# Expert weights in six places instead of four, one set of statistics for Mamba's two norms, tanh in place of sigmoid, in an eight-layer network on one core

## What is computed

```python
def _layernorm(x, axis=-1, eps=1e-05):
    m = jnp.mean(x, axis=axis, keepdims=True)
    v = jnp.var(x, axis=axis, keepdims=True)
    return (x - m) / jnp.sqrt(v + eps)
...
# layer 1
r = jax.nn.sigmoid(jnp.einsum('btc,dc->btd', xr, W_r))
...
# layer 2, whose input x is the layernorm above
h = (x - mu) * lax.rsqrt(var + LN_EPS) * ln_g + ln_b
...
return x + out
...
# layer 6
x_in = jax.nn.silu(xz[..., :D]) * jax.nn.sigmoid(xz[..., D:])
...
out = out * jax.lax.rsqrt(jnp.mean(out * out, axis=-1, keepdims=True) + eps) * norm_w
...
# layer 7, for the two best of eight experts of each token
g = jnp.einsum('nd,edf->enf', xt, w_gate) + b_gate[:, None, :]
u = jnp.einsum('nd,edf->enf', xt, w_up) + b_up[:, None, :]
h = jax.nn.silu(g) * u
y = jnp.einsum('enf,efd->end', h, w_down) + b_down[:, None, :]
```

## Time and profile before

| | us |
|---|---|
| median of 3 runs | 1400.7 |
| lowest and highest run | 1398.04 and 1400.92 |
| span of the profiled execution | 1400.6 |
| PE busy in it | 1104.8 (79%) |
| DVE, ACT, POOL busy | 890.9, 630.4, 281.7 |

### The profile page before, as it was taken

How to read it: one execution, slowest core, us unless ns; L and a number is a source line. 1 busy time by engine, 2 the same in 40 slices (tenths; PEclk the granted TensorE clock), 3 DMA queues, 4 the chain that set the end, 5 groups by cost and what they waited for, 6 DMA issues and landing times.

```text
span 1400.6 us, 15057 instructions
## 1 busy us (share of the span) xinstructions
PE 1104.8 (79%) x4959; PEld 698.7 (50%) x4959; DVE 890.9 (64%) x1919; ACT 630.4 (45%) x1194; POOL 281.7 (20%) x258
## 2 busy tenths in 40 slices
PE   4978657767977979686768676799999899897791
PEld 2536312334743634353457442574555556787781
DVE  6787879987558767767635789723735652363432
ACT  3433385424552348634237972273252434542330
POOL 3000113324120002130230244202000032014404
PEclk9999877777989999878889897999999999899996
DMA  8100000003520000000125420370000014468782
GB/s 322 47 0 1 0 0 0 0 1 118 163 61 1 0 0 1 0 0 0 45 92 177 131 74 21 96 224 21 1 1 0 1 63 132 157 214 283 260 277 69
DMA packets 49411, 107.02 MB, mean 76 GB/s; under 512 B 4840, under 2 KB 32368, under 8 KB 48688
## 3 DMA queue, kind: packets, MB, share of 16 engines
q1 hardware_dynamic: 44656, 92.74, 20.7%
q0 software_dynamic: 4096, 8.40, 2.0%
q10 hardware_dynamic: 576, 4.87, 0.8%
HBM read 91.24 MB, written 14.75 MB: 76 GB/s over the span
## 4 chain that ended last, share of the span: by engine, by line
PE 41%; DVE 22%; ACT 13%; issue 9%; POOL 7%; DMA 6%; SPq 1%; DVEq 0%; POOLq 0%; ACTq 0%
PE ps L1920 6%; PE ps L1638 5%; DMA expert_ring<-in_e_dram 4%; PE ps L1586 4%; PE ps L1752 4%; DVE up L1341 3%; PE ps L1858 3%; POOL slots_dram L717 3%; ACT big L957 2%; PE ps L1692 2%; PE ps L1829 2%; PE ps L1958 2%; DVE big L1348 2%; POOL up L727 2%; PE ps L1909 1%
## 5 line engine op out<-in xcount | busy, mean ns | idle before, releaser
L1858 PE MATMUL ps<-big,expert_ring 128*128 128x128 f32 x1160 | 158.0, 286 | 33.6 <-DMA expert_ring<-in_e_dram 20.4
L1858 PEld LDWEIGHTS ps<-big,expert_ring 128*128 128x128 f32 x1160 | 145.2, 199 | 48.0 <-DMA expert_ring<-in_e_dram 26.9
L1341 DVE TENSOR_TENSOR_SCAN up<-cv,big 128x512 f32<-128x512 f32 x128 | 152.5, 1230 | 21.5 <-ACT cv L908 17.4
L660 POOL TENSOR_TENSOR rstd<-ve,nhalf 128x4 f32<-128x4 f32 (+1 forms) x41 | 47.2, 1153 | 577.2 <-DVE ve L1119 470.6
L1752 PE MATMUL ps<-big,consts 128*128 128x512 f32 x256 | 154.3, 735 | 2.4 <-DVE big L1348 2.4
L697 POOL TENSOR_TENSOR big<-big,mt 128x512 f32<-128x512 f32 x64 | 85.8, 1344 | 279.1 <-ACT mt L901 152.6
L1920 PE MATMUL ps<-big,weights 128*128 128x512 f32 x256 | 115.4, 597 | 0.0
L1769 PE MATMUL ps<-q,row_pick 96*128 96x512 bf16 x128 | 54.5, 448 | 76.6 <-DVE big L1348 61.4
L1829 PE MATMUL ps<-expert_ring,big 128*128 128x128 f32 x792 | 107.6, 280 | 5.9 <-ACT big L957 3.6
L1829 PEld LDWEIGHTS ps<-expert_ring,big 128*128 128x128 f32 x792 | 98.9, 195 | 15.3 <-ACT big L957 9.8
L1459 DVE SCALAR_TENSOR_TENSOR big<-ps,expert_ring,key 128x128 f32<-128x128 f32 x184 | 51.8, 344 | 79.6 <-PE ps L1858 67.4
(11 more groups left out here) (247 smaller groups left out, 1943.4 us busy)
## 6 DMA issues: line engine op xcount, KB each, us to landing
expert_ring<-in_e_dram SPq DMA_DIRECT2D x46, 836.0 KB, 5.3
expert_ring<-in_e_dram SPq DMA_DIRECT2D x53, 578.0 KB, 4.4
big<-slots_dram SPq DMA_DIRECT2D x21, 256.0 KB, 3.5
results_dram<-mt SPq DMA_DIRECT2D x21, 256.0 KB, 5.3
weights<-in_w_dram ACTq DMA_DIRECT2D x1, 3072.0 KB, 15.5
slots_dram<-big SPq DMA_DIRECT2D x2, 1024.0 KB, 10.3
weights<-in_w_dram SPq DMA_DIRECT2D x1, 1600.0 KB, 8.6
x<-in_x_dram SPq DMA_DIRECT2D x4, 256.0 KB, 13.6
```

The lines of the kernel that those rows point to most:

```text
L1341: dve.tensor_tensor_scan(UP[s][:, j, PAD:PAD + T], CV[s][:, j, :], BIG2[s][:, j, :], 0.0, ALU.mult, ALU.add).then_inc(m_scan[s], 1)
L1858: last = pe.matmul(bank4(s, r if m else b % 2)[:, k, :], ring[:, q % RING, r * T + k * P:r * T + (k + 1) * P], XGT[s][:, b // 4 % 4, b % 4 ...
```

## The change

It has five parts. No turn moves: `RUNS` and `PLAYS` are as before.

1. **Two more places for expert weights**, used in layer 7 alone. They lie in the columns of `weights` that held the weights of layers 0 and 1. `ring_plan` gives each load the place whose block is longest ago; once all six are in use, a load of layer 7 waits for the block six loads back. The first load into each of the two places waits for the end of layer 1 in sequences 2 and 3.
2. **SP reads the expert's number before it waits for the place**, in both expert layers; before, it waited first.
3. **Banks**: in stream 1's layer 7, odd blocks use banks 0 and 1 of stream 0. The gate and up halves wait for block b-2 instead of b-1, and block 1 waits for stream 0's last product.
4. **Mamba's norms**: both come from the statistics of X. With variance v, the inner norm of the outer is X minus its mean times (v(1+eps)+eps^2)^-0.5, and this one is written first; statistics of `XN` are not taken.
5. **tanh for sigmoid**: sigmoid(a) = (1 + tanh(a/2)) / 2. DVE multiplies by 1 + tanh in the same instruction; the half goes into layer 1's addition to x, and in layer 6 into two tables of weights that DVE halves once, at the end of layer 4 of sequence 0, and into a constant.

```diff
+SPARE = 2
...
+def ring_plan():
+
+    order, held, used, plan = expert_loads(), [None] * (RING + SPARE), [0] * (RING + SPARE), {}
+    place = {load: k for k, load in enumerate(order)}
+    for load in order:
+        slots = range(RING + SPARE * load[0])
+        slot = min(slots, key=lambda k: -1 if held[k] is None else place[held[k]])
+        used[slot] += 1
+        plan[load] = slot, used[slot], held[slot]
+        held[slot] = load
+    return plan
...
+        plan = ring_plan()
+
+        def expert_slot(m, s, b):
+
+            slot = plan[m, s, b][0]
+            if slot < RING:
+                return ring[:, slot, :]
+            return W[:, (slot - RING) * EW[1]:(slot - RING + 1) * EW[1]]
...
+        def expert_bank(m, s, r, b):
+
+            if m and s % NS == 1 and b % 2:
+                return bank(s - 1, r)
+            return bank(s, r if m else b % 2)
...
-                            q = loads.index((m, s, n))
+                            slot, _, previous = plan[m, s, n]
                             if n == 0:
                                 sp.wait_ge(g.eb[s], g.eb.at(s, 0))
-                            if q >= RING:
-                                pm, pi, pb = loads[q - RING]
+                            e = sp.value_load(whoi[s][0:1, n:n + 1], min_val=0, max_val=NE - 1)
+                            if previous:
+                                pm, pi, pb = previous
                                 sp.wait_ge(moe[pm].y[pi], moe[pm].y.at(pi, pb))
-                            e = sp.value_load(whoi[s][0:1, n:n + 1], min_val=0, max_val=NE - 1)
+                            elif slot >= RING:
+                                for i in range(NB - NS, NB):
+                                    sp.wait_ge(x_done[1][i], x_done[1].at(i, 0))
                             src = (e3_d if m else e1_d)[bass.ds(e, 1)].rearrange("o p n -> p (o n)")
-                            sp.dma_start(ring[:, q % RING, 0:EW[m]], src).then_inc(ring_in[q % RING], 16)
+                            sp.dma_start(expert_slot(m, s, n)[:, 0:EW[m]], src).then_inc(ring_in[slot], 16)
                             continue
...
-                yield from ln(n2o, s)
-                yield from ln(n2, s)
+                for n, at in ((n2, NC), (n2o, 0)):
+                    yield
+                    pool.wait_ge(n.var[s], n.var.at(s, 0))
+                    pool.tensor_tensor(rstd[s][:, at:at + NC], ve[s][:, at:at + NC], nhalf[:, 0:NC], ALU.pow)\
+                        .then_inc(n.rs[s], 1)
...
-                act.activation(BIG1[s][:, 6, :], bank(s, 1), ACT.Sigmoid).then_inc(f0_sg[s], 1)
+                act.activation(BIG1[s][:, 6, :], bank(s, 1), ACT.Tanh, scale=0.5).then_inc(f0_sg[s], 1)
...
-                    act.activation(UP[s][:, j, PAD:PAD + T], bank(s, 2 + j), ACT.Sigmoid).then_inc(s_slg[s], 1)
+                    act.activation(UP[s][:, j, PAD:PAD + T], bank(s, 2 + j), ACT.Tanh, scale=0.5)\
+                        .then_inc(s_slg[s], 1)
...
-                step(dve.tensor_tensor(b[:, 7, :], bank(s, 2), b[:, 6, :], ALU.mult))
-                add_x(s, b[:, 7, :].rearrange("p (c n) -> p c n", c=NC), x_done[1])
+                step(dve.scalar_tensor_tensor(b[:, 7, :], b[:, 6, :], 1.0, bank(s, 2), ALU.add, ALU.mult))
+                dve.scalar_tensor_tensor(X[s][:, :, :], b[:, 7, :].rearrange("p (c n) -> p c n", c=NC), 0.5, X[s][:, :, :],
+                                         ALU.mult, ALU.add).then_inc(x_done[1][s], 1)
 
             def mamba(s):
                 yield
                 dve.wait_ge(x_done[1][s], x_done[1].at(s, 0))
-                yield from norm(n2o, s, (X[s], XN[s]))
-                yield
-                dve.wait_ge(n2o.done[s], n2o.done.at(s, 0))
-                yield from norm(n2, s, (XN[s], XH[s]))
+                for c in range(NC):
+                    last = dve.bn_stats(stat[s][:, c, 0, :], X[s][:, c, :])
+                step(last)
+                for c in range(NC):
+                    last = dve.bn_aggr(mv[s][:, c, :], stat[s][:, c, 0, :])
+                step(last)
+
+                dve.tensor_scalar(ve[s][:, NC:2 * NC], mv[s][:, 0:NC, 1], 1.0 + LN_EPS, LN_EPS * LN_EPS, ALU.mult,
+                                  ALU.add).then_inc(n2.var[s], 1)
+                dve.tensor_scalar(ve[s][:, 0:NC], mv[s][:, 0:NC, 1], LN_EPS, None, ALU.add).then_inc(n2o.var[s], 1)
+                for n, at, dst in ((n2, NC, XH[s]), (n2o, 0, XN[s])):
+                    yield
+                    dve.wait_ge(n.rs[s], n.rs.at(s, 0))
+                    for c in range(NC):
+                        last = dve.tensor_scalar(dst[:, c, :], X[s][:, c, :], mv[s][:, c, 0:1],
+                                                 rstd[s][:, at + c:at + c + 1], ALU.subtract, ALU.mult)
+                    last.then_inc(n.done[s], 1)
+                yield
...
+                if s == 0:
+                    dve.wait_ge(wsem[3], 16)
+                    dve.tensor_scalar(w("s_abc"), w("s_abc"), 0.5, None, ALU.mult)
+                    dve.tensor_scalar(pr("normw", 0, 2), pr("normw", 0, 2), 0.5, None, ALU.mult)
...
-                    dve.tensor_tensor(BIG1[s][:, j, :], CV[s][:, j, :], UP[s][:, j, PAD:PAD + T], ALU.mult)\
-                        .then_inc(s_xi[s], 1)
+                    dve.scalar_tensor_tensor(BIG1[s][:, j, :], UP[s][:, j, PAD:PAD + T], 1.0, CV[s][:, j, :],
+                                             ALU.add, ALU.mult).then_inc(s_xi[s], 1)
...
-                dve.tensor_scalar(ve[s][:, 0:NC], bank(s, 3)[:, 0:NC], 1.0 / 256, RMS_EPS, ALU.mult, ALU.add)\
+                dve.tensor_scalar(ve[s][:, 0:NC], bank(s, 3)[:, 0:NC], 1.0 / 1024, RMS_EPS, ALU.mult, ALU.add)\
...
-                        q = loads.index((m, s, b))
+                        slot, use, _ = plan[m, s, b]
                         for r in range(m + 1):
                             yield
                             if r == 0:
-                                pe.wait_ge(ring_in[q % RING], 16 * (q // RING + 1))
+                                pe.wait_ge(ring_in[slot], 16 * use)
                                 if b % 4 == 0:
                                     pe.wait_ge(g.gt[s], g.gt.at(s, b // 4))
-                                if m and b:
-                                    pe.wait_ge(g.act[s], g.act.at(s, b - 1))
-                            elif b:
-                                pe.wait_ge(g.h[s], g.h.at(s, b - 1))
+                            free = g.h if r else g.act
+                            if m and s % NS == 1 and b == 1:
+                                pe.wait_ge(g.h[s - 1], g.h.at(s - 1, NBLK - 1))
+                            elif m and b > s % NS:
+                                pe.wait_ge(free[s], free.at(s, b - 1 - s % NS))
                             for k in range(4):
-                                last = pe.matmul(bank4(s, r if m else b % 2)[:, k, :],
-                                                 ring[:, q % RING, r * T + k * P:r * T + (k + 1) * P],
+                                last = pe.matmul(expert_bank(m, s, r, b)[:, k * P:(k + 1) * P],
+                                                 expert_slot(m, s, b)[:, r * T + k * P:r * T + (k + 1) * P],
                                                  XGT[s][:, b // 4 % 4, b % 4 * P:(b % 4 + 1) * P], start=True, stop=True)
                             last.then_inc(g.up[s], 1)
                         if b:
```

25 lines of the change are left out of this document (11 added, 14 removed).

## The result

| | before | after |
|---|---|---|
| median, us | 1398.04 (5 runs, 1387.58 to 1400.92) | 1380.85 (5 runs, 1380.52 to 1387.33) |
| ratio to before | | 0.9895, 95% interval 0.9869 to 0.992 |
| span of the profiled execution, us | 1400.6 | 1385.5 |

Two more pairs, from two later batches, gave 0.9903 (0.9876 to 0.9929) and 0.9902 (0.987 to 0.9935). So the change makes the kernel 1.0% faster, 14 us.

What follows compares the result with a forecast made beforehand. The prediction took a chain across engines as the bound, in late layer 7 the four weight places; -4.8 - 2.8 - 0.7 - 1.2 - 0.9 - 0.5 + 0.6 = -10.3 us gave 1390.4, range 1384.5 to 1398 (the forecast's own 1387 to 1394).

Steps and rivals of the forecast that it cites:

- The period, -4.8: Layer 7, stream 1, blocks 10 to 22: six places shorten each interval from 3.35 to 2.95 us, -4.8 us over 12.
- The equation with 2 T in it: Layer 7 with four places: 4 T = 2 T + 0.6 + 0.7 + 5.3, so a block takes 3.3 us.
- The start of stream 1: Layer 7: the last scatter lands sooner, -2.5 us, and a wait before stream 1's routing shrinks, -0.3; together -2.8.
- block 10: Layer 7, stream 1: its load w10 leaves 1.7 us sooner after the second output store, so it starts 0.7 us earlier.
- The read before the wait, -1.2: Layer 3: 0.55 us saved on each of four loads on the chain, bounds 0 and -2.2, taken as -1.2 us.
- Mamba's norms, -0.9: Sequence 0: XH written earlier and statistics dropped, so PE's transposes come 0.9 us sooner; bounds 0 and -1.3.
- tanh, -0.5: Twelve table loads leave ACT, but only PE's 0.49 us wait at 1023.76 is on the chain: -0.5 us.
- +0.6: Added DVE work: halving weights and parameters, 0.35 us, and slower three-operand multiplications; +0.6 us, bounds 0 and +1.5.
- PE alone is the bound: Rival: every gain reaches its far end, -15.3 us in all, so 1385.4 us; chance 0.18.
- The wires give no more: Rival: loads slow as more are in flight, layer 7's interval stays at 3.35 us, so 1395.2 us; chance 0.18.
- the places are not used: Rival: SP stands before its stores whenever a place is free; only edits outside layer 7 count, 1398.7 us; chance 0.08.
- The small transfers: Rival, layer 7: scatter, store and gathers queue behind two more loads, costing 15.4 us, so 1409 us; chance 0.06.

Runs made afterwards that it cites:

- turns_later: The changed kernel with stream 0's last turns on DVE and SP moved behind more of stream 1's blocks; 1374.57 us, ratio 0.9823 to before.
- before_third: The kernel before, unchanged, run again for a third trace; 1396.29 us, ratio 0.9996 to before.
- small_only: The kernel before with only Mamba's norms and tanh for sigmoid changed; 1396.30 us, ratio 0.9988 to before.
- after_third: The changed kernel, unchanged, run again for a third trace; 1384.43 us, ratio 0.9902 to before.
- no_bank: The changed kernel with the banks undone, so odd blocks of stream 1 use its own banks; 1379.49 us, ratio 0.9872 to before.
- no_read: The changed kernel with SP reading the expert's number after the wait again; 1385.99 us, ratio 0.9927 to before.
- five: The changed kernel with five places for layer 7's weights instead of six; 1384.90 us, ratio 0.9913 to before.
- tanh_only: The kernel before with only tanh for the sigmoids; 1419.87 us, ratio 0.9992 to before.
- places_only: The kernel before with only the added places and the banks; 1406.07 us, ratio 0.9923 to before.
- norms_only: The kernel before with only Mamba's norms changed; 1419.05 us, ratio 0.998 to before.
- three: The changed kernel with three places for layer 7's weights instead of six; 1432.56 us, ratio 1.026 to before.

## Why the prediction was wrong

The measured time is 9.5 us under the forecast. In steps: the forecast subtracted 10.3 from 1400.7; from the later median of before, 1398.04, the same sum gives 1387.7, and 2.7 of the 9.5 are this base. The ratio 0.9895 puts the kernel at 1383.4, that is 14.7 less where the sum has 10.3: 4.3 more. The last 2.5 us are that four of its five runs came within 0.8 us of each other at the low end, at a granted clock of 0.896, with the fifth at 1387.33 and 0.889.

**The range is the step that failed first.** Its lower end was put together from the bounds of the terms, -7.2, -3.4 and so on, and nothing was in it for the spread of executions or for the base. With every term at its far bound, the norms at -1.3 and the additions at 0 too, the sum is -16.3 and the time 1384.4, which is where the range ended. Yet the three runs shown were 2.9 us apart, before's five later spanned 13.3, and one trace of a kernel stands up to 8 us from another ahead of layer 7.

**The period, -4.8.** The right size, by luck, for a reason that was half wrong. Three traces of before take 12 intervals of 3.19 on average, three of after 2.78: -4.9. I had started from 3.35, a high one, and ended at 2.95, also too high. The step that failed is "two bounds that coincide are not both reached at once". The 334 GB/s was the mean of a window and no bound. Before's own trace has more over 8 us of that window:

```profile
1263.00:1271.00 8.00, 6.02 (x52) 5.64 (x51) 2.65 (x10) 2.42 (x10) 5.97 (x7) 1.00 1.05 386
```

At the 369 GB/s of turns_later the wires need 2.5 us for a block, an estimate from the prediction's 0.92 MB, so PE's 2.68 alone is the bound, and PE ran without a gap at it. The equation with 2 T in it fitted 3.3 by chance. The result comes 3.75 us behind the start of the next block, so three intervals, not two, must cover some 9.3 us (3.75, 0.74 to issue, a median of 4.8 to land in the first trace). That is 3.1 with four places, and 2.9 with the number read first.

**The start of stream 1 and block 10, -2.8 and -0.7.** Together they are -2.7 for -3.5, but the two terms were split wrongly. On the chips where before takes 1396 to 1401 us there are three traces with four places and the turns unmoved (before, before_third, small_only) and five with more (after, after_third, no_bank, no_read, five). From 1235.75 to stream 0's second output store they take 84.2 and 83.0 us on average: -1.3 for my -2.8. The last scatter does land in 5.1 to 5.4 us with four places and in 2.3 to 4.3 with more, and stream 1's first block comes 1.8 sooner on average, but little more than 1 us of it reaches the store. From that store to block 10 they take 7.8 and 6.4: -1.4 for my -0.7. As forecast, w10 leaves 1.5 us behind the store in all five, where it took 2.5 to 4.0, and in after it lands at 1318.38, just ahead of block 10 at 1318.43.

**The read before the wait, -1.2.** The local gain in layer 3 is there, and by 918 us it can no longer be told from 0. In one pair of traces the loss stands at a wait for tokens that comes through POOL, and in the clock. With four places the read is worth 2 us in the last stretch (12 intervals of 0.17), with six at most 1. So -1.2 is neither borne out nor refuted for the whole change; what failed is the reason "Behind three of them ACT or PE soon has work of its own queued", which looked no further than the next work.

**Mamba's norms, -0.9, and tanh, -0.5.** -1.2 for the one, just inside my bound of -1.3. Of tanh I had one place; there were three, -0.7, -0.35 and -0.9, the last given back. "Elsewhere PE or DVE is the later one" was too quick: at 1087.52 the load stands between the projection and the gate just as at 1020.48. The halvings take 0.25 and 0.16 us on DVE at 485.8 in after. Between 470 and 503 us the ten traces of the changed kernel and of the kernels made from it are 0.6 us longer than the first of before, but small_only and tanh_only only 0.1, and kernels without tanh lie between -0.4 and +0.5. The three-operand multiplications show in no stretch. So the +0.6 is neither shown nor excluded.

**What the trace carries and what stays open.** Layer 7 gives -7.6 (forecast -8.3), the pieces ahead of it that repeat give -1.2 - 0.7 - 0.35 = -2.3 (forecast -2.0). That is -9.9 against the -14 of three ratios, whose intervals each reach 3.5 to 4.5 us to either side. Part of the other 4 us may stand ahead of layer 7 and not in stretches that repeat: at 1175 us the nine traces whose kernels have parts 2, 4 and 5 are 9.4 us ahead of the first trace of before on average (4.9 to 13.8), the four of before and places_only 5.3 (0 to 7.9). The difference of 4.1 has a standard error of 2.1, so it holds the 2.3 as well as all that is missing. The single parts sum to -10.9 - 0.9 - 2.8 - 1.1 = -15.7 by their times, so the times agree with each other, and norms_only has the largest excess, 1.6 over what its trace shows. A higher clock is not what the two later pairs show: the mean granted clock of the changed kernel's executions is 0.883 and 0.890, that of before's 0.885 and 0.892. Where the rest comes from stays open.

**The rivals.** "PE alone is the bound", 1385.4, is what happened behind block 11, and it is the case nearest to the time; its other terms did not all reach their far ends. "The wires give no more" and "the places are not used" are refuted by three, five and the windows. The small transfers did not queue: scatters land sooner, the store takes 7.19 for 7.57. The Trainium skill ("Perfetto Trace Analysis", section Roofline) says that a core whose neighbour is idle can pull more than the 358 GB/s that I had quoted from its page "DMA: Bandwidth & Descriptors"; the 369 GB/s of turns_later agree.
